# Second attention of an eight-head block: low-half score products paired across two heads, three score banks, single maxima

## The reference, cut to what matters

```
x = x + proj(attention_1(norm(x)))           # first attention, with a learned position bias
t = tokens of x                              # [8, 1024, 256]
q, k, v = split(norm(t) @ W + b)             # second attention, 8 heads of 32
qk = einsum('bhqd,bhkd->bhqk', q, k)
qe = einsum('bhqd,qkd->bhqk', q, E[i - j + 1023])   # sinusoidal embedding of the distance
t = t + softmax((qk + qe) / sqrt(32)) @ v
t = t + experts(norm(t))                     # Sinkhorn routing, top-k, 8 experts
```

## Time and profile before

| | us |
|---|---|
| median of 3 runs | 2886.26 |
| lowest, highest | 2875.22, 2887.24 |
| profiled execution, its own time | 2896.32 |
| its span, first to last instruction | 2894.5 |
| TensorE busy | 2541.5 (88%) |
| VectorE busy | 2021.5 (70%) |
| GpSimd busy | 1971.0 (68%) |
| ScalarE busy | 1403.8 (48%) |
| mean granted TensorE clock | 0.937 |

### The profile page before, as it was taken

How to read it: one execution, slowest core, us unless ns; L and a number is a source line. 1 busy time by engine, 2 the same in 40 slices (tenths; PEclk the granted TensorE clock), 3 DMA queues, 4 the chain that set the end, 5 groups by cost and what they waited for, 6 DMA issues and landing times. The chain is left out here.

```text
span 2894.5 us, 47510 instructions
## 1 busy us (share of the span) xinstructions
PE 2541.5 (88%) x18598; PEld 867.1 (30%) x18598; DVE 2021.5 (70%) x3096; ACT 1403.8 (48%) x2558; POOL 1971.0 (68%) x767
## 2 busy tenths in 40 slices
PE   7899999999999999969889999999999999761265
PEld 2564222222222222235542222222222222240145
DVE  3475787787787877857876777777777777578144
ACT  4345555555555555523335555555555555440012
POOL 2123888888888888854447888878878878630763
PEclk8899999999999999989999999999999999875567
DMA  3994212222212312259764222233222232260337
GB/s 73 230 234 142 49 49 49 74 66 52 49 49 70 71 49 52 49 165 303 233 213 102 48 63 48 63 88 70 63 48 63 63 88 55 89 190 7 94 122 244
DMA packets 239568, 284.13 MB, mean 98 GB/s; under 512 B 65014, under 2 KB 172790, under 8 KB 236014
## 3 DMA queue, kind: packets, MB, share of 16 engines
q1 hardware_dynamic: 228848, 255.85, 33.0%
q0 software_dynamic: 6144, 16.85, 1.9%
q10 hardware_dynamic: 4352, 8.39, 0.8%
HBM read 171.32 MB, written 110.47 MB: 97 GB/s over the span
## 5 line engine op out<-in xcount | busy, mean ns | idle before, releaser
L849 POOL TENSOR_TENSOR room_af<-room_af 128x2048 f32<-128x2048 f32 x160 | 725.4, 4534 | 163.9 <-ACT room_af L821 149.7
L1197 POOL TENSOR_TENSOR bias<-bias 128x2048 f32<-128x2048 f32 x160 | 724.6, 4529 | 147.9 <-ACT bias L1169 134.0
L984 DVE TENSOR_REDUCE row_min_kf<-PS 128x1 f32<-128x1024 f32 x532 | 627.5, 1220 | 269.5 <-PE PS L976 268.0
L631 DVE CUSTOM_DVE_ANT_0 PS<-PS,bias 128x1024 f32<-128x1024 f32 x532 | 644.2, 1241 | 164.3 <-PE PS L619 147.6
L1169 ACT ACTIVATE bias<-PS 128x512 f32<-128x512 f32 x1024 | 557.2, 597 | 411.9 <-PE PS L1095 410.9
L821 ACT ACTIVATE room_af<-PS 128x512 f32<-128x512 f32 x1024 | 555.7, 595 | 397.3 <-PE PS L743 397.3
L1095 PE MATMUL PS<-stacks_kf 128*128 128x512 f16 x2048 | 532.9, 383 | 8.4 <-PEq L87 8.3
L736 PE MATMUL PS<-QS_af,KS_af 128*128 128x512 f16 x1024 | 333.8, 387 | 11.2 <-PEq L87 4.5
L1095 PEld LDWEIGHTS PS<-stacks_kf 128*128 128x128 f16 x2048 | 157.1, 97 | 448.8 <-ACT bias L1169 292.1
L769 PE MATMUL PS<-room_af,V_af 128*32 128x512 f32 x2048 | 272.8, 605 | 0.3 <-ACT room_af L821 0.3
L1115 PE MATMUL PS<-bias,V_kf 128*32 128x512 f32 x2048 | 272.7, 605 | 0.0
(11 more groups left out here) (183 smaller groups left out, 2874.8 us busy)
## 6 DMA issues: line engine op xcount, KB each, us to landing
stacks_kf<-query_key_halves SPq DMA_DIRECT2D x119, 256.0 KB, 7.3
query_key_halves<-bias SPq DMA_DIRECT2D x32, 768.0 KB, 4.3
query_key_halves<-room_af SPq DMA_DIRECT2D x32, 512.0 KB
KS_af<-query_key_halves SPq DMA_DIRECT2D x51, 256.0 KB, 4.7
QS_af<-query_key_halves SPq DMA_DIRECT2D x51, 256.0 KB, 6.9
V_kf<-values SPq DMA_DIRECT2D x9, 1024.0 KB, 10.7
V_af<-values SPq DMA_DIRECT2D x17, 512.0 KB, 8.8
stacks_kf<-query_key_halves SPq DMA_DIRECT2D x68, 128.0 KB, 9.4
```

What stands on the lines that cost most here:

```text
L631: nc.vector.tensor_tensor_reduce(out=max_ps[n % len(max_ps)], in0=max_ps[n % len(max_ps)], in1=bias_h[:, g * HG + j, z:z + N], scale=-1.0, ...
L849: nc.gpsimd.tensor_tensor(acc[:, u % 2], so_far, prob[:, n % PR], ALU.add).then_inc(acc_ok, 1)
L984: nc.vector.tensor_reduce(row_min[:, m:m + 1], max_ps[n % len(max_ps)], AX.X, ALU.min).then_inc(max_read, 1)
L1197: nc.gpsimd.tensor_tensor(acc[:, u % 2], so_far, prob[:, n % PR], ALU.add).then_inc(acc_ok, 1)
```

## The change

In the second attention:

- The low-half operands leave `stacks` for a tile `lows` in which two heads stand above each other, heads 0 and 2 in rows 0 to 63, heads 1 and 3 in rows 64 to 127. The low product of a head has 64 rows, the maximum among them: it takes the place of one table row, whose slow remainder goes to the high product (`SLOW`, the table and `rot` are shifted for it). No zero rows are left, and `fill_rows` fills one small tile.
- `scores(s)` now does two heads: two full KHL x QHH matmuls, then two 64-row matmuls in the two row halves, adding to the same two banks. There are three score banks; the bank of the denominators is given up for it.
- The order of a step becomes: scores of heads 0 and 1; all maxima jobs but the last; the weighing of step n - 1; scores of heads 2 and 3; the last maximum.
- The denominators are one block of 12 fp32 matmuls (24 instructions in a trace) at step 1, behind the last maximum, into a bank of `max_ps`, as a job between the maxima; VectorE copies the sums (`take_sums`) and takes reciprocals in place, from step 2 on. FIN becomes 5, TAKE stays 1.
- 15 transfers per group instead of 11, 20 for the tables instead of 10; 4 for `edram` instead of 2.

```diff
@@ constants, banks
-                QHH, KHL, QL, KH1 = range(4)
-                LEAD = 2 * D
-                stacks = tile("stacks", [P, 2, 4, HG, N], F16)
+                QHH, KHL = range(2)
+                QL, KH1 = range(2)
+                LAST = 2 * D - 1
+                stacks = tile("stacks", [P, 2, 2, HG, N], F16)
+                lows = tile("lows", [P, 2, 2, HG // 2, N], F16)
...
-                score_ps = [PS[:, 4 + i, :] for i in range(2)]
-                out_ps = PS[:, 6, :]
-                den_ps = PS[:, 7, :]
+                score_ps = [PS[:, 4 + i, :] for i in range(3)]
+                out_ps = PS[:, 7, :]
...
-                LOADS = 16 * 11
+                LOADS = 16 * 15
...
-                DEN, REC, TAKE, FIN = 2, 3, 1, 4
+                DEN, REC, TAKE, FIN = 1, 2, 1, 5
@@ load_group
+                    for h in range(2):
+                        for first, st, s, rows in ((0, QL, 1, D), (D, QL, 3, D - 1), (0, KH1, 4, D)):
+                            first += 2 * D * h
+                            sp.dma_start(lows[first:first + rows, q % 2, st], src[0:rows, s, h:HG:2]).then_inc(stk[q % 2], 16)
@@ fill_rows
-                    zeros = [(words(stacks[LEAD:P, q, st]), 0.0) for q in range(2) for st in (QL, KH1)]
-                    ones_ = [(stacks[LEAD:LEAD + 1, q, KH1], W1S * W1S) for q in range(2)]
...
+                    nc.gpsimd.memset(den_w[:], 1.0).then_inc(fill, 1)
@@ tensor: scores
-                                if s >= 2:
-                                    pe.wait_ge(exps, s - 1)
-                                for n, (k_, q_) in enumerate(((KHL, QHH), (KH1, QL))):
-                                    last = nc.tensor.matmul(score_ps[s % 2], stacks[:, slot, k_, j, kt * P:(kt + 1) * P],
-                                                            stacks[:, slot, q_, j, first:first + CH], start=(n == 0), stop=(n == 1))
-                                last.then_inc(full, 1)
+                                for i in range(2):
+                                    if s + i >= 3:
+                                        pe.wait_ge(exps, s + i - 2)
+                                    nc.tensor.matmul(score_ps[(s + i) % 3], stacks[:, slot, KHL, j + i, kt * P:(kt + 1) * P],
+                                                     stacks[:, slot, QHH, j + i, first:first + CH], start=True, stop=False,
+                                                     skip_group_check=True)
+                                for i in range(2):
+                                    half = slice(2 * D * i, 2 * D * (i + 1))
+                                    nc.tensor.matmul(score_ps[(s + i) % 3], lows[half, slot, KH1, j // 2, kt * P:(kt + 1) * P],
+                                                     lows[half, slot, QL, j // 2, first:first + CH], start=False, stop=True,
+                                                     skip_group_check=True).then_inc(full, 1)
@@ tensor: denominators
+                            def denominators(n, u):
+                                pe.wait_ge(max_read, n - 1)
+                                pe.wait_ge(acc_ok, ADDS * (u + 1))
+                                parts = [prob[:, (KTU * u + kt) % PR] for kt in range(ADDS + 1, KTU)] + [acc[:, u % 2]]
+                                for i, part_ in enumerate(parts):
                                     for j in range(HG):
...
+                                last.then_inc(max_full, 1)
@@ tensor: order of a step
                                 if n < NU * KTU:
                                     scores(HG * n)
-                                    scores(HG * n + 1)
-                                    maxima(n)
-                                    scores(HG * n + 2)
-                                    scores(HG * n + 3)
+                                    maxima(step_jobs[n][:-1])
                                 if 1 <= n <= NU * KTU:
                                     weigh(n - 1)
+                                if n < NU * KTU:
+                                    scores(HG * n + 2)
+                                    maxima(step_jobs[n][-1:])
                                 if n >= KTU and n % KTU == DEN:
-                                    denominators(n // KTU - 1)
+                                    denominators(job_at[(n // KTU - 1, "den")], n // KTU - 1)
@@ gpsimd: finish
+                                if u >= 1:
+                                    pool.wait_ge(fin, u)
@@ vector
+                            def take_sums(n, u):
+                                dve.wait_ge(max_full, n + 1)
                                 if u >= 2:
                                     dve.wait_ge(scaled, u - 1)
...
+                                nc.vector.tensor_copy(rec[:, u % 2, :], max_ps[n % 2][:, 0:CH]).then_inc(max_read, 1)
@@ token phase 1, turned_high
-                            nc.scalar.copy(stg[:, u % 2, g, 2, :], rf[:, (u * G + g) % 2, :]).then_inc(r_high, 1)
+                            nc.scalar.activation(stg[:, u % 2, g, 2, :], rf[:, (u * G + g) % 2, :], ACT.Copy,
+                                                 scale=bcol[:, 2 * G:2 * G + 1]).then_inc(r_high, 1)
```

More of the change, by code:

```diff
@@ L28, in build @@
     WS = 64.0
-    W1S = 16.0
     QS = float(D) ** -0.5
@@ L939, in load_group @@
                     src = batch(qk_dram[1], b)[:, g].rearrange("a s (j d) n -> d (a s) j n", d=D)
-                    for r, st, s in ((0, QHH, 0), (1, QHH, 2), (2, QHH, 0), (3, QHH, 2), (0, QL, 1), (1, QL, 3), (0, KH1, 4)):
-                        sp.dma_start(stacks[r * D:(r + 1) * D, q % 2, st], src[:, s]).then_inc(stk[q % 2], 16)
+                    for r, s in ((0, 0), (1, 2), (2, 0)):
+                        sp.dma_start(stacks[r * D:(r + 1) * D, q % 2, QHH], src[:, s]).then_inc(stk[q % 2], 16)
+                    for first, s, rows in ((3 * D, 2, slice(0, D - 1)), (4 * D - 1, 3, slice(D - 1, D))):
+                        sp.dma_start(stacks[first:first + rows.stop - rows.start, q % 2, QHH], src[rows, s]).then_inc(stk[q % 2], 16)
+                    for h in range(2):
+                        for first, st, s, rows in ((0, QL, 1, D), (D, QL, 3, D - 1), (0, KH1, 4, D)):
+                            first += 2 * D * h
+                            sp.dma_start(lows[first:first + rows, q % 2, st], src[0:rows, s, h:HG:2]).then_inc(stk[q % 2], 16)
                     for r, c, s in ((0, 0, 4), (2, 0, 5), (0, 1, 5), (2, 1, 4)):
@@ L960, in move_maxima @@
                     for j in range(HG):
-                        sp.dma_start(stacks[LEAD:LEAD + 1, slot, QL, j, first:first + CH].rearrange("p (t n) -> p t n", n=P),
+                        row = j % 2 * 2 * D + LAST
+                        sp.dma_start(lows[row:row + 1, slot, QL, j // 2, first:first + CH].rearrange("p (t n) -> p t n", n=P),
                                      max_row[j * TT:(j + 1) * TT, u % 2, :]).then_inc(m_in[u % 2], 16)
@@ L995, in attention_keys_first @@
                 job_at, jobs_done = {}, 0
-                for n in range(NU * KTU):
-                    for job in step_jobs[n]:
-                        job_at[job] = jobs_done
+                for n in range(NU * KTU + DEN + 1):
+                    if n < NU * KTU:
+                        for job in step_jobs[n]:
+                            job_at[job] = jobs_done
+                            jobs_done += 1
+                    if n >= KTU and n % KTU == DEN:
+                        job_at[(n // KTU - 1, "den")] = jobs_done
                         jobs_done += 1
@@ L1118, in weigh @@
                                                             skip_group_check=True)
-                                if kt > ADDS:
-                                    if kt == ADDS + 1 and u >= 1:
-                                        pe.wait_ge(recd, PIECES * u)
-                                    for j in range(HG):
-                                        last = nc.tensor.matmul(den_ps[j * D:(j + 1) * D, :], den_w[:], prob[:, n % PR, j, :],
-                                                                start=(kt == ADDS + 1), stop=False, skip_group_check=True)
-                                last.then_inc(weighed, 1)
-                            def denominators(u):
-                                pe.wait_ge(acc_ok, ADDS * (u + 1))
-                                for j in range(HG):
-                                    last = nc.tensor.matmul(den_ps[j * D:(j + 1) * D, :], den_w[:], acc[:, u % 2, j, :],
-                                                            start=False, stop=True, skip_group_check=True)
-                                last.then_inc(den, 1)
+                                last.then_inc(weighed, 1)
+                            def denominators(n, u):
[3 more added lines that the diff above has]
+                                for i, part_ in enumerate(parts):
+                                    for j in range(HG):
```

(16 more changed lines are left out.)

69 lines of the change are left out of this document (39 added, 30 removed).

## The result

The changed kernel takes 3124.18 us (3120.38 to 3124.94, four runs) against 2886.06 (2875.22 to 2887.24) of the kernel before on the same chip: ratio 1.083, interval 1.080 to 1.086. It is 238 us slower. The direction was forecast, the size was not: +62 us was the forecast, and the time lies 146 us above the range.

A forecast was written before the change was run, and what follows sets the result against it. TensorE was taken to bound the second attention; a unit of 32.64 us against 30.70 gave +60 us over 31 unit boundaries, plus 2 outside the attention: 2886 + 62 = 2948 us, range 2910 to 2978.

The forecast's parts named there:

- Low pair B to low pair A: From the low products of heads 2 and 3 to the next step's of heads 0 and 1: 1.44 us.
- the plain step: A second-attention step without take, denominators or transpose: 3.52 us forecast, against 3.47 before the change.
- the take step: Once a unit, the first weighing waits for ScalarE's copy of the old sums: 1.63 us more, step 5.15.
- the transpose: Transpose of the maxima in step 6, waiting 0.17 us for a reduction: 0.5 us added, step 4.02.
- The unit: 512 queries of four heads, eight steps of the second attention: 32.64 us forecast against 30.70.
- Wait 1: Pair A's second key matmul waits for the preceding pair B's first exponential to free its bank: 0.36 us a step.
- the term for the transfers: SP's 10 more table transfers and 4 more per group, 0.5 us each: 0 to 6 us, taken as 2.
- The cover of 21 us: In the steady stage a group's loads have six steps (21 us) before use, hiding 2 us more.
- the saving of the array: Four full low-half products become two side-by-side pairs: 0.43 us less TensorE work in each step.
- The rivals: TensorE never waits, 2868 (0.07); no change, 2888 (0.10); low pairs not side by side, 3058 (0.03); maxima's row late, 2998 (0.03).
- sign of being wrong: Plain step near 3.16, take's step no longer than others, or low pair and maximum taking 0.97 us.
- the maxima's row lands late: Rival: the maxima's row transfers land after the next unit's first key matmul; up to 50 us, 2998; chance 0.03.

The follow-up runs named there:

- e1: The changed kernel with the group loads' 31 query rows sent as 16 + 15 and the low query rows as 32: 2993.3 us, ratio 1.034.
- e3: As e2, with TAKE = 0, so ScalarE copies the old sums one step earlier: 2899.2 us, ratio 1.0013.
- e6: As e3, with both maxima of a step behind its second pair of heads: 2872.9 us, ratio 0.998.
- e7: As e3, with both maxima of a step behind its first pair of heads: 2935.6 us, ratio 1.019.
- e2: As e1, with the tables' 31 rows also loaded as 16 + 15, 28 table transfers instead of 20: 2963.6 us, ratio 1.023.
- e4: The kernel before, with two of its eleven loads of a group cut into 31 + 1 rows: 3077.2 us, ratio 1.062.
- e9: As e6, with the denominators between the two maxima and the maxima's transpose behind the second pair, ahead of the maxima: 2838.1 us, ratio 0.986.
- e5: The changed kernel with TAKE = 0 alone, its 31-row loads left as they are: 3092.5 us, ratio 1.074.

## Why the prediction was right or wrong

**Right: what the order of TensorE does.** Low pair B to low pair A takes 1.40 us (2125.28 to 2126.68), 1.44 was said; the plain step 3.47 for 3.52; the weighing of the take step follows low pair A after 2.12 for 2.17; the denominators' block takes 2.72 for 2.71; a pair with its maximum 0.54; a low pair takes 0.22 (2123.20 to the maximum at 2123.43), as one matmul did. In e1, where no stack is late, the steps from weighing to weighing are 3.99 for 4.02 with the transpose (1998.83 to 2002.82), 5.06 for 5.15 with the take (2009.76 to 2014.82) and 5.86 for 5.87 with the denominators (to 2020.68). The unit without a late transfer or a fallen clock is 32.25 for 32.64. The take's place and cost were as forecast, and e3 takes it away by one constant. Wait 1 is confirmed by e6 and e7, whose plain steps come out within 0.05 of what it gives.

**Wrong: the term for the transfers.** The step that failed reads: "SP gets 10 more table transfers and 4 more per group, at 3.46 / 7 = 0.5 us each ... In the steady stage a group's loads have six steps (21 us) before use, so 2 more are hidden." It took each new transfer at the issue time of an old one, all of 32 rows. By e1 the group's loads cost 142 us (124 in the attention, 19 in token phase 1, by the stage lengths), and by e2 the tables 31 more. Together 173, where 2 stood. Of the 124, 89 are the 16 waits themselves. What is left in token phase 1 of e2 against before is 7 us, of the size that the term had priced. The cover of 21 us was sound for loads that go out in 6 us; it wasn't held against one that takes 10 us to move and holds up those behind it. e4 shows this without the rest of the change.

**Wrong: no price for the clock.** Behind the take's wait the granted clock is at half, the 1.2 GHz level, for most of 3.6 us (second row, 0.53), and the same behind the wait for the stacks (first row, 0.50; the clock is the column ahead of the DMA share):

```profile
2115.00:2118.50 3.50, 3.50 (x14) 0.46 (x14) 1.22 (x1) 0.00 (x0) 1.29 (x2) 0.50 0.00 0
2128.80:2132.40 3.60, 3.60 (x14) 0.41 (x14) 0.00 (x0) 0.21 (x1) 0.00 (x0) 0.53 0.00 0
```

A fall behind the take makes a unit 33.84 instead of 32.25. By e3 it comes to 15 us over the stage. Behind the stacks, from weighing to weighing TensorE takes 4.98 (2115.29 to 2120.27) where a plain step takes 3.47; this half clock is part of the 142.

**The sum.** By the runs in their order, as differences of the ratios times 2886, each good to about 10 us: group loads 142, tables 31, take with its clock 63, and +4 left in e3, which makes the 240 (1.083 of 2886). The forecast's +62 was mostly the take, with wait 1 eating the saving of the array; e2, which keeps both and has no load of 31 rows, stands at +67. The unit was put 0.39 us too high, 12 us over 31 units, and the clock, 15 us, was not in the sum: that the two nearly cancel is luck. The rivals played no part, for none had a slow transfer, and no sign of being wrong in the forecast looked at one; "the maxima's row lands late" looked at the right class of cause and the wrong transfer.

**Open.** The busy share and the rate show one engine's work in the flats; no row names the engine. What 15 rows alone get wasn't measured, only that 16 + 15 cost nothing that shows. Why SP's queue stays held while such a transfer is on its way (12.15 us for six issues) wasn't taken apart.

## What to carry to other kernels

Look at the row count of every transfer that a change cuts or adds: 31 rows cost more than all else here, and 16 + 15, or a full 32 with one row overwritten later, cost next to nothing. A matmul saved ahead of a bank that its reader has not yet freed only buys waiting; put independent work (here both maxima) inside the reader's delay, which with the denominators set between them turned an even kernel (e3) into one 1.4% faster (e9). When TensorE's weighing moves ahead, move the copy that frees its bank ahead too, and count the half clock behind a stall with the stall.

## What the runs showed of the hardware beyond what was expected

- While only transfers of 31 rows are under way, 25 GB/s move at a busy share of 0.07 of the 16 DMA engines, and SP's six issues around two of them take 12.15 us, against 2.79 where none has 31 rows (e1).
- The same wait of 1.5 us was followed by a fall of the clock in some units and not in others: in e1 the weighing behind it lasts 1.07 at 2014.82 and 1.92 at 2176.14. Waits of 0.36 in every step (e7) cost no clock: its mean is 1.00 and all its units are 32.20.
- A slow load costs less when TensorE is slow for another reason, and more when that is mended: e5 got back 28 us where e3 got 63.
